# A two-layer graph network on one core: in-degrees, W2's low parts and a score weight placed elsewhere in the order of work

## The chip, the core and the metric

The kernel runs on one core of a Trainium2 chip. The core's engines work side by side, each through its own queue in order: TensorE (PE) for matmuls and transposes, VectorE (DVE), ScalarE (ACT), GpSimd (POOL), and SyncE (SP), which here only issues DMAs. They wait for one another through semaphores. The metric is the device time of one execution in microseconds, lower is better.

## The reference

A graph of 1250 nodes (rows of 768 numbers) and 40000 edges goes through two residual blocks. The first is a graph attention network of two layers, the second a graph convolution network of two layers.

```python
h = relu(layernorm(x))
# layer 1 of the attention network, 4 heads of 512 columns; layer 2: 1 head of 768
def gat(x, W, a_src, a_dst, bias):
    h = (x @ W).reshape(N, H, C)
    e = leaky_relu(al_s[src] + al_d[dst], 0.2)   # al_s = <h, a_src>, al_d = <h, a_dst>
    ex = exp(e - segment_max(e, dst)[dst])
    out = segment_sum(h[src] * (ex / segment_sum(ex, dst)[dst]), dst)
    return out + bias
x = x + gat(elu(gat(h, W1, ...)), W2, ...)
h = relu(layernorm(x))
def gcn(x, W, b):
    h = x @ W
    deg = segment_sum(ones, dst); dinv = where(deg > 0, rsqrt(deg), 0)
    return segment_sum(h[src] * (dinv[src] * dinv[dst])[:, None], dst) + b
x = x + gcn(relu(gcn(h, G1, c1)), G2, c2)
```

Every node has a loop to itself as well. The in-degrees `deg` are needed only by the convolution network, that is in the second half of the kernel.

## The kernel before, in words

The edges become a dense table `counts` of how often each source points to each destination: 10 tiles of 128 sources by 1280 destinations, 16-bit integers. All sums over edges are then matmuls against weights made from this table.

To keep float32 accuracy, every matmul is done three times: each operand is split in a high part (a rounded copy, made by ScalarE) and a low part (the difference, made by VectorE), and high x high, high x low and low x high are added up in PSUM.

The work goes in this order. First x is normalised and multiplied with W1 for all heads (30 row tiles written to memory, the last ten, of head 0, kept on chip). Then come the four heads. A head has five chunks of up to 256 destinations; with q the number of the chunk over all heads (0 to 19), TensorE does for each q the products of chunk q - 2 with W2 (`products`, four pieces: two row tiles by two halves of the columns, in two banks of PSUM, so the third piece waits until VectorE has added the first to the rows), and then the sums over sources of chunk q (`sums`). Between the sums stand two `turn_out` transposes of chunk q - 1, at s = 3 and s = 6; the second waits for the low part of the first, `elu_lo`. The weights of a chunk are made in five groups of two source tiles: ScalarE's `exps`, VectorE's `weigh`, ScalarE's `hi`, VectorE's `lo`, through two buffers and a ring of five slots. VectorE also finds each head's maxima over the masked scores (`take_top`, one instruction a source tile), adds products (`add_products`), divides (`normalize`), finishes elu (`elu_out`, `elu_lo`) and splits W2's rows (`split_weights`: in the second chunk of a head, c = 1, four instructions for W2's four blocks of that head). Head 0 has no earlier head to lie beside, so its maxima are found while TensorE is still at the last ten tiles (`row_lo` and `row_hi` split those); after them TensorE turns the maxima (`turn_top`, after tile 4), the shift (`turn_shift`, after tile 5) and broadcasts it (`spread_first`, after tile 6). `first_slopes` makes the score weights of W2's four blocks for the first head, W2 times the attention vectors.

After the heads comes the second attention layer, made by the same `Weights` object from chunk number `SECOND` = 20 on. Between the layers TensorE has to wait for the first weights of the new layer. Then the convolution network follows.

The in-degrees are nine additions over the tiles of `counts` on VectorE (`degree_sums`), two conversions on ScalarE (`degrees_out`) and 20 matmul records with a column of ones on TensorE (`degrees`, after the last tile); VectorE copies the result to `deg`.

The order on every engine is written out by hand in the program; nothing plans it. All waits are counts on semaphores. Lines: `exps` L250, `weigh` L267 and L269, `hi` L258, `lo` L276, `degree_sums` L1039, `row_lo` L1045, `take_top` L1056 and L1058, `first_slopes` L966, `row_hi` L687, `degrees_out` L698, `degrees` L1469, `split_weights` L716 (ScalarE) and L1101 (VectorE), `normalize` L1114 and L1122, `elu_lo` L1138, `add_products` L1151, `second_lo` L1177, `turn_out` L1517, `sums` L1535, `products` L1565, the second layer's sums L2080.

Of the kernel before, what the change touches and what calls it, by code (L numbers as in the profile page):

```python
# [6 lines left out]
fp32 = mybir.dt.float32  # L7
# [79 lines left out]
class Memory:  # L87

    def __init__(self, nc, keep):
# [50 lines left out]
        self.deg_sum = late("deg_sum", [P, NP], u16)  # L140
# [160 lines left out]
def first_layer(nc, st, mem, x, src, dst, W2, b1, as2, ad2, h_scratch, w_in, a_in, load_weights, load_vectors, tile_in, later):  # L301
# [15 lines left out]
    deg_sum = mem.deg_sum  # L317
    LATE = 3 * G * CW * 4
    deg_f = [Area(nc, mem.at_weights + at + LATE, mem.at_x)(f"deg_f{j}", [P, NP // 2], fp32)
             for j, at in enumerate((WEIGHT_BYTES - RING_BYTES, WEIGHT_BYTES - RING_BYTES // 2))]  # L320
# [99 lines left out]
    b1bc = sbx("b1bc", [P, HA], fp32)  # L420
    w2_st = sbx("w2_st", [P, 2, D], fp32)
    w2 = [sbx("w2_hi", [P, KH, DS], f32r), sbx("w2_lo", [P, KH, DS], f32r)]
    a2bc = sbx("a2bc", [P, 2, D], fp32)
    second = mem.rows_all[:, :, D], al02[:, :, 0]
# [19 lines left out]
    W2v = W2.rearrange("(i p) n -> p i n", p=P)  # L444
    SECOND = HEADS * NC
# [59 lines left out]
    with nc.Block() as block:  # L505
        @block.sync
        def _(sp):
# [44 lines left out]
            for h in range(HEADS):  # L552
# [3 lines left out]
                if h + 1 < HEADS:  # L556
# [9 lines left out]
                    load_bias(h + 1)  # L566
            half.sync(sp)

        @block.gpsimd
        def _(pool_):  # L570
# [38 lines left out]
            pool_.wait_ge(deg_f_ready, 2)  # L609
# [7 lines left out]
        def _(act):  # L617
# [77 lines left out]
            def degrees_out():  # L695
                act.wait_ge(d_step, T - 1)
                for j in range(2):
                    nc.scalar.activation(deg_f[j][:, :], deg_sum[:, j * NP // 2:(j + 1) * NP // 2], ACT.Copy).then_inc(deg_f_ready, 1)  # L698
# [36 lines left out]
            for h in range(HEADS):  # L735
                scores = al[:, :, h], al02[:, :, h]
                for c in range(NC):
                    q = h * NC + c
                    last, second_last = before(q, 1), before(q, 2)
                    for g in range(NG):  # L740
# [5 lines left out]
                        if q == 0 and g == 1:  # L746
                            degrees_out()
                        if q == 0 and g == NG - 1:
                            act.wait_ge(deg_done, 1)
# [20 lines left out]
            for dt in range(NDT):  # L770
                elu_hi(SECOND - 2, dt)

# [25 lines left out]
        def _(dve):  # L798
# [236 lines left out]
            def degree_sums(tiles):  # L1035
                for t in tiles:
                    if t >= 2:
# [28 lines left out]
            for k in range(KH):  # L1066
# [14 lines left out]
            shift_parts(nc, chain, mem, dest_scores(0), lambda: dve.wait_ge(reduced, 1), shift_ready)  # L1081
            row_lo(5)
            dve.wait_ge(shift_t, 1)
            nc.vector.tensor_copy(shiftT[:, 0, :], p_s0).then_inc(shift_out, 1)
            degree_sums(range(1, 5))
            row_lo(6)
            degree_sums(range(5, 7))
# [125 lines left out]
            for h in range(HEADS):  # L1213
                final = h == HEADS - 1
                for c in range(NC):
                    q = h * NC + c
                    last, second_last = before(q, 1), before(q, 2)
                    for g in range(NG - 1):
# [8 lines left out]
                        if q == 0 and g == 0:  # L1227
                            row_lo(T - 3)
                            degree_sums(range(7, T))
                        if g >= 1:  # L1230
                            wt.lo(nc, dve, q, c, g - 1)
                        if second_last is not None and g == 1:
                            elu_lo(second_last, 1)
                        if q == 0 and 1 <= g <= 2:
                            row_lo(T - 3 + g)
                        if q == 0 and g == 2:
                            dve.wait_ge(deg_done, 1)
# [1020 lines left out]
```

## Time and profile before

| | us |
|---|---|
| three runs | 1159.08, 1156.29, 1159.99 (median 1159.08) |
| profiled execution | 1161.38, span 1159.5 |
| TensorE busy (96% of the span) | 1113.2 |
| VectorE busy (73%) | 850.5 |
| ScalarE busy (44%) | 512.3 |
| GpSimd busy (2%) | 27.5 |

The rows further down have the start of an instruction in us from the span's start, its duration, engine, source line and operation, and what it writes and reads. In square brackets stands how long the engine was idle before it, and which instruction released it. A row may merge several instructions (x10). The granted clock is TensorE's, as a share of 2.4 GHz.

### The profile page before, as it was taken

Reading aid. Unit: us, or ns where it says so; the run is one execution under the profiler, and the core shown is the slowest. Engines: PE = TensorE matmul, PEld = TensorE weight load, DVE = VectorE, ACT = ScalarE, POOL = GpSimd, SP = SyncE. Lnnn points to the kernel's source line nnn. Section 1 sums busy time; section 2 is a strip of 40 time slices with the busy share of each in tenths; the row PEclk is TensorE's granted clock in tenths of the full one; section 3 lists DMA queues with packets and bytes.
Section 4 is the critical chain, followed back from the end, with each engine's and each line's share of the span. In section 5 each row is a group of like instructions: output and inputs, shape, how many; then the busy total and the mean of one; then the engine's idle time right before and its main releaser. Section 6 shows DMA issues by size and latency. Waiting matters only on the chain.

```text
span 1159.5 us, 17646 instructions
## 1 busy us (share of the span) xinstructions
PE 1113.2 (96%) x7126; PEld 1044.8 (90%) x7126; DVE 850.5 (73%) x1431; ACT 512.3 (44%) x1056; POOL 27.5 (2%) x40
## 2 busy tenths in 40 slices
PE   5999999988999999999999999989999999999998
PEld 4878886788999999999999999979998999899998
DVE  7998898888879888898879777689777533341263
ACT  4232322276446655575446665255537521431110
POOL 4200000020000000000000000000000000000000
PEclk9999999998999999999999999989999999999999
DMA  6134232021003100201003000031012200100321
GB/s 234 53 120 114 71 128 73 1 64 55 1 29 100 34 23 14 90 25 55 1 28 101 29 1 1 1 123 52 28 56 79 82 1 2 28 14 1 134 83 52
DMA packets 29347, 63.17 MB, mean 54 GB/s; under 512 B 3684, under 2 KB 6344, under 8 KB 29264
## 3 DMA queue, kind: packets, MB, share of 16 engines
q1 hardware_dynamic: 29072, 61.68, 16.5%
q8 instruction: 60, 0.98, 0.3%
q10 hardware_dynamic: 192, 0.32, 0.1%
q14 instruction: 23, 0.19, 0.1%
HBM read 46.45 MB, written 15.54 MB: 53 GB/s over the span
## 4 chain that ended last, share of the span: by engine, by line
PE 68%; DVE 7%; DMA 1%; ACT 1%; issue 1%; DVEq 0%; ACTq 0%
PE banks L1535 20%; PE banks L1565 14%; PE banks L2080 9%; PE banks L2203 6%; PE banks L2196 5%; PE banks L2145 5%; PE banks L2119 4%; PE banks L1517 2%; DVE top L1058 1%; ACT e L250 1%; DMA w_st<-in_L_gnn_W 1%; PE banks L235 1%; DVE pf L269 1%; DVE e L267 1%; DVE w_lo L1101 0%
## 5 line engine op out<-in xcount | busy, mean ns | idle before, releaser
L1535 PE MATMUL banks<-hs,ring_hi 128*128 128x258 f32 (+1 forms) x1600 | 303.0, 290 | 4.3 <-DVE z L1122 4.3
L1535 PEld LDWEIGHTS banks<-hs,ring_hi 128*128 128x128 f32 (+1 forms) x1600 | 250.8, 190 | 6.2 <-DVE z L1122 4.5
L1535 PE MATMUL banks<-hs,ring_lo 128*128 128x258 f32 (+1 forms) x800 | 228.3, 285 | 0.0
L250 ACT ACTIVATE e<-banks,al 128x256 f32<-128x256 f32 (+1 forms) x450 | 180.5, 494 | 8.4 <-PE banks L235 8.4
L258 ACT ACTIVATE ring_hi<-pf 128x512 fp32r<-128x512 f32 (+1 forms) x125 | 81.7, 653 | 173.0 <-DVE pf L269 169.9
L1535 PEld LDWEIGHTS banks<-hs,ring_lo 128*128 128x128 f32 (+1 forms) x800 | 152.0, 190 | 0.0
L1565 PE MATMUL banks<-w_hi,oT_hi 128*128 128x386 f32 (+3 forms) x320 | 109.4, 342 | 3.4 <-DVE shiftT L1211 3.2
L1565 PE MATMUL banks<-w_lo,oT_hi 128*128 128x386 f32 (+3 forms) x320 | 108.7, 340 | 0.0
L1565 PE MATMUL banks<-w_hi,oT_lo 128*128 128x386 f32 (+3 forms) x320 | 108.2, 338 | 0.0
L267 DVE TENSOR_TENSOR e<-e 128x512 f32<-128x512 f32 (+1 forms) x125 | 84.6, 677 | 24.9 <-ACT e L250 24.6
L1409 PE MATMUL banks<-w_hi,xT_hi 128*128 128x512 f32 x240 | 96.7, 403 | 1.3 <-DVE xT_lo L879 0.8
L1409 PE MATMUL banks<-w_hi,xT_lo 128*128 128x512 f32 x240 | 93.7, 390 | 0.0
L1409 PE MATMUL banks<-w_lo,xT_hi 128*128 128x512 f32 x240 | 93.7, 390 | 0.0
L269 DVE SCALAR_TENSOR_TENSOR pf<-e,counts 128x512 f32<-128x512 f32 (+1 forms) x125 | 84.9, 680 | 4.3
L276 DVE TENSOR_TENSOR ring_lo<-pf,ring_hi 128x512 fp32r<-128x512 f32 (+1 forms) x125 | 84.3, 674 | 4.5 <-ACT ring_hi L258 2.1
L891 DVE TENSOR_TENSOR hot<-codes,parts_of 125x1300 bf16<-125x1300 uint16 x97 | 74.0, 827 | 5.2 <-PE banks L1422 5.2
L2080 PE MATMUL banks<-hs_hi,ring_hi 128*128 128x386 f32 x200 | 70.9, 354 | 6.1 <-DVE hs_lo L1177 4.6
L2080 PE MATMUL banks<-hs_lo,ring_hi 128*128 128x386 f32 x200 | 69.2, 346 | 0.0
L2203 PE MATMUL banks<-z_hi,d_hi 128*128 128x384 f32 (+1 forms) x200 | 67.6, 338 | 0.0
L2203 PE MATMUL banks<-z_lo,d_hi 128*128 128x384 f32 (+1 forms) x200 | 67.6, 338 | 0.0
L1151 DVE TENSOR_TENSOR rows<-rows,banks 128x384 f32<-128x384 f32 (+2 forms) x80 | 44.2, 552 | 31.6 <-PE banks L1565 30.7
L2080 PE MATMUL banks<-hs_hi,ring_lo 128*128 128x386 f32 x200 | 66.3, 337 | 0.0
(273 smaller groups left out, 2129.0 us busy)
## 6 DMA issues: line engine op xcount, KB each, us to landing
w_st<-in_L_gnn_W SPq DMA_DIRECT2D x26, 384.0 KB, 3.2
h_scratch<-stage SPq DMA_DIRECT2D x30, 256.0 KB, 2.0
hs<-h_scratch SPq DMA_DIRECT2D x30, 256.0 KB, 2.9
w_st<-in_L_gnn_W SPq DMA_DIRECT2D x4, 1536.0 KB, 7.4
gw_st<-in_L_gnn_W SPq DMA_DIRECT2D x12, 384.0 KB, 4.0
xr<-in_x SPq DMA_DIRECT2D x9, 384.0 KB, 10.2
rows<-in_x SPq DMA_DIRECT2D x9, 384.0 KB, 3.9
x_scratch<-rows SPq DMA_DIRECT2D x9, 384.0 KB
```

What stands on the lines that cost most here:

```text
L250: last = nc.scalar.activation(self.e[:, local % 2, a, i, 0:n], self.p_shift[:, a, 0:n], ACT.Exp, bias=scores[a][:, g * G + i:g * G + i + 1])
L258: nc.scalar.activation(self.ring[0][:, g, :, 0:n], self.pf[:, (c * NG + g) % 2, :, 0:n], ACT.Copy)\
L267: nc.vector.tensor_tensor(e[:, 0], e[:, 0], e[:, 1], ALU.max).then_inc(self.e_max, 1)
L269: nc.vector.scalar_tensor_tensor(out=self.pf[:, local % 2, :, 0:n], in0=e[:, 0], scalar=1.0, in1=counts[:, g * G:(g + 1) * G, d0:d0 + n], ...
L276: nc.vector.tensor_tensor(self.ring[1][:, g, :, 0:n], self.pf[:, (c * NG + g) % 2, :, 0:n], self.ring[0][:, g, :, 0:n].bitcast(fp32), ALU. ...
L891: nc.vector.tensor_tensor(hot[:, wd % SLOTS, :, :, :].rearrange("e a i (v t) -> e (a i) v t", t=2), codes[:, :, :, :].rearrange("e a i (v ...
L1409: last = nc.tensor.matmul(p_h[n % 2], xT[a][:, k, t * P:(t + 1) * P], w[b][:, k, :], start=u == 0, stop=u == 3 * KD - 1)
L1535: last = nc.tensor.matmul(p_a[0:m, dt, half, 0:HH], wt.ring[a][:, s // G, s % G, dt * P:dt * P + m], hs[:, s, b, half * HH:(half + 1) * HH ...
L1565: last = nc.tensor.matmul(p_g[i % 2][0:m, 0:cols.stop - cols.start], oT[a][:, k, dt * P:dt * P + m], w2[b][:, k, cols], start=j == 0, stop ...
L2080: last = nc.tensor.matmul(p_a(t)[0:m, half, 0:AH], wt.ring[a][:, s // G, s % G, dt * P:dt * P + m], hs[b][:, s, half * AH:(half + 1) * AH] ...
L2145: last = nc.tensor.matmul(p_f(f)[:, 0:n], w1[a][:, k, f * P:(f + 1) * P], yT[b][:, k, 0:n], start=u == 0, stop=u == len(terms) - 1)
L2203: last = nc.tensor.matmul(p_q(d)[0:m, half, :], d_hi[0:k, d % 2, s, 0:m], z[a][0:k, s, half * HALF:(half + 1) * HALF], start=s == 0 and a ...
```

## The change

Five edits, all of order and place; the arithmetic is the same.

1. `degree_sums` leaves the first head. Its nine steps stand in chunks 1 to 4 of the last head, between the additions of products (list `DEGREES`). The sums and their float copies lie where the W2 staging and the attention vectors were.
2. `degrees_out` on ScalarE stands behind the heads, `degrees` on TensorE behind the broadcast of the second layer's first shift. VectorE copies the result behind the third weighing of that layer. The waits for them in the first head, on all engines, go; SP waits for the degrees before the second half's loads.
3. `first_slopes` of the fourth block stands behind `shift_parts` and no longer ahead of the maxima.
4. VectorE's `split_weights` for blocks 2 and 3 stands in the third chunk (c = 2, after group 1) and no longer at the end of the second. ScalarE's part stays.
5. GpSimd's memset of the rows no longer waits for the degrees.

```diff
--- before.py
+++ after.py
@@ -137,7 +137,6 @@
         late = Area(nc, self.at_late, end)
         self.abc = late("abc", [P, 2, HID], fp32)
         self.stage = late("stage", [P, 2, HID], fp32)
-        self.deg_sum = late("deg_sum", [P, NP], u16)
         self.junk = edges("junk", [P, 2, HID], bf16)
         self.edges = edges
         self.e_i = edges("e_i", [EP, 2, EJ, EC], i32)
@@ -314,10 +313,6 @@
     stage, junk = mem.stage, mem.junk
     al_row = sbp("al_row", [NV, NP], fp32)
     vr = [sbp("v_hi", [P, KD, NV], f32r), sbp("v_lo", [P, KD, NV], f32r)]
-    deg_sum = mem.deg_sum
-    LATE = 3 * G * CW * 4
-    deg_f = [Area(nc, mem.at_weights + at + LATE, mem.at_x)(f"deg_f{j}", [P, NP // 2], fp32)
-             for j, at in enumerate((WEIGHT_BYTES - RING_BYTES, WEIGHT_BYTES - RING_BYTES // 2))]
     top0 = sbp("top0", [P, NP], fp32)
     early = Area(nc, sbp.at, mem.at_weights + 26 * 1024)
     a2_first = early("a2_first", [P, 2, D], fp32)
@@ -418,9 +413,13 @@
     ev = sbx("ev", [P, NDT, HID], fp32)
     pos = sbx("pos", [P, NDT, HID], fp32)
     b1bc = sbx("b1bc", [P, HA], fp32)
+    at_w2_st = sbx.at
     w2_st = sbx("w2_st", [P, 2, D], fp32)
     w2 = [sbx("w2_hi", [P, KH, DS], f32r), sbx("w2_lo", [P, KH, DS], f32r)]
+    on_a2, on_w2 = Area(nc, sbx.at, sbx.at + 2 * D * 4), Area(nc, at_w2_st, at_w2_st + 2 * D * 4)
     a2bc = sbx("a2bc", [P, 2, D], fp32)
+    deg_sum = on_a2("deg_sum", [P, NP], u16)
+    deg_f = [on_a2("deg_f0", [P, NP // 2], fp32), on_w2("deg_f1", [P, NP // 2], fp32)]
     second = mem.rows_all[:, :, D], al02[:, :, 0]
     second_dest = mem.rows_all[:, :, D + 1], al02[:, :, HEADS]
 
@@ -442,6 +441,7 @@
     a2_early, w2_early = sem("a2_early"), [sem(f"w2_early{k}") for k in range(KH)]
     v2hi_done, v2lo_done = sem("v2hi_done"), sem("v2lo_done")
     W2v = W2.rearrange("(i p) n -> p i n", p=P)
+    DEGREES = [(), (1, 2, 3), (4, 5), (6, 7), (8, 9)]
     SECOND = HEADS * NC
     FIRST_COLS, REST_COLS = slice(0, CW), slice(CW, NP)
     p_first = banks[:, 6, 0:NDT * P].rearrange("p (k c) -> p k c", c=P)
@@ -564,6 +564,7 @@
                         sp.wait_ge(wt.used, (h + 1) * (NC * NG) + (t // G + 1))
                         sp.dma_start(hs[:, t, 1, 0:HID].bitcast(fp32), h_scratch[h + 1, :, t, :]).then_inc(tile_in[t], 16)
                     load_bias(h + 1)
+            sp.wait_ge(deg_done, 1)
             half.sync(sp)
 
         @block.gpsimd
@@ -606,7 +607,6 @@
             nc.gpsimd.memset(b1bc[:, HID:HA], 0.0).then_inc(ones_done, 1)
             for j in range(2):
                 pool_.wait_ge(spilled[j], 16 * (FIRST // 2))
-            pool_.wait_ge(deg_f_ready, 2)
             nc.gpsimd.memset(mem.rows_all[:, :, :], 0.0).then_inc(zeroed, 1)
 
             pool_.wait_ge(hi2_done, 6)
@@ -694,6 +694,7 @@
 
             def degrees_out():
                 act.wait_ge(d_step, T - 1)
+                act.wait_ge(w2lo_done, HEADS * KH)
                 for j in range(2):
                     nc.scalar.activation(deg_f[j][:, :], deg_sum[:, j * NP // 2:(j + 1) * NP // 2], ACT.Copy).then_inc(deg_f_ready, 1)
 
@@ -743,10 +744,6 @@
                             elu_hi(second_last, 0)
                         if q == 0 and g <= 2:
                             row_hi(T - 3 + g)
-                        if q == 0 and g == 1:
-                            degrees_out()
-                        if q == 0 and g == NG - 1:
-                            act.wait_ge(deg_done, 1)
                         if g >= 1:
                             wt.hi(nc, act, q, c, g - 1)
                         if second_last is not None and g == 1:
@@ -769,6 +766,7 @@
                         split_weights(h, range(2, KH))
             for dt in range(NDT):
                 elu_hi(SECOND - 2, dt)
+            degrees_out()
 
             def second_hi(t):
                 act.wait_ge(wt.used, (SECOND + 1) * NG)
@@ -1034,6 +1032,8 @@
 
             def degree_sums(tiles):
                 for t in tiles:
+                    if t == 1:
+                        dve.wait_ge(v2_done, 2 * KH * HEADS)
                     if t >= 2:
                         dve.wait_ge(d_step, t - 1)
                     nc.vector.tensor_tensor(deg_sum[:, :], counts[:, 0, :] if t == 1 else deg_sum[:, :], counts[:, t, :],
@@ -1063,7 +1063,7 @@
                     ins.then_inc(top_step, 1)
                     n_top[0] += 1
 
-            for k in range(KH):
+            for k in range(KH - 1):
                 first_slopes(k)
             row_lo(0)
             dve.wait_ge(al_done, 1)
@@ -1079,12 +1079,11 @@
             dve.wait_ge(top_t, 1)
             nc.vector.tensor_reduce(mem.amax[:, :], p_top0[:, 0:T, :], AX.X, ALU.max).then_inc(reduced, 1)
             shift_parts(nc, chain, mem, dest_scores(0), lambda: dve.wait_ge(reduced, 1), shift_ready)
+            first_slopes(KH - 1)
             row_lo(5)
             dve.wait_ge(shift_t, 1)
             nc.vector.tensor_copy(shiftT[:, 0, :], p_s0).then_inc(shift_out, 1)
-            degree_sums(range(1, 5))
             row_lo(6)
-            degree_sums(range(5, 7))
 
             def split_rows(h, g):
                 if h == 0:
@@ -1226,16 +1225,14 @@
                             elu_lo(second_last, 0)
                         if q == 0 and g == 0:
                             row_lo(T - 3)
-                            degree_sums(range(7, T))
                         if g >= 1:
                             wt.lo(nc, dve, q, c, g - 1)
                         if second_last is not None and g == 1:
                             elu_lo(second_last, 1)
+                        if c == 2 and g == 1:
+                            split_weights(h, range(2, KH))
                         if q == 0 and 1 <= g <= 2:
                             row_lo(T - 3 + g)
-                        if q == 0 and g == 2:
-                            dve.wait_ge(deg_done, 1)
-                            nc.vector.tensor_copy(deg[:, :], p_d).then_inc(deg_done, 1)
                         if c == 0 and 1 <= g <= 2:
                             split_rows(h, g - 1)
                         if c == NC - 1 and not final and g == NG - 2:
@@ -1249,6 +1246,8 @@
                             add_products(second_last, range(1))
                             if c == NC - 2 and not final:
                                 weight_slope(h + 1, 2, 0)
+                            if final:
+                                degree_sums(DEGREES[c][0:1])
                             add_products(second_last, range(1, 2))
                     if c == 0:
                         split_rows(h, 2)
@@ -1256,6 +1255,8 @@
                         weight_slope(h + 1, 3, 0)
                     if not final:
                         next_top(h, c, 0)
+                    else:
+                        degree_sums(DEGREES[c][1:2])
                     if second_last is not None:
                         add_products(second_last, range(2, 3))
                     if c == NC - 1 and not final:
@@ -1264,6 +1265,8 @@
                         next_top(h, c, 1)
                     elif c >= 2:
                         second_top((c - 2) * NDT)
+                    else:
+                        degree_sums(DEGREES[c][2:3])
                     if second_last is not None:
                         add_products(second_last, range(3, NB))
                     if c == 0:
@@ -1278,8 +1281,6 @@
                     wt.lo(nc, dve, q, c, NG - 1)
                     if c == 0:
                         split_rows(h, NG - 1)
-                    if c == 1:
-                        split_weights(h, range(2, KH))
                     if c == NC - 2 and not final:
                         weight_slope(h + 1, 2, 1)
                     if c == NC - 1 and not final:
@@ -1331,6 +1332,8 @@
             second_lo(5)
             wt.lo(nc, dve, SECOND, 0, 1)
             wt.weigh(nc, dve, counts, SECOND, 0, 2)
+            dve.wait_ge(deg_done, 1)
+            nc.vector.tensor_copy(deg[:, :], p_d).then_inc(deg_done, 1)
             second_lo(6)
             second_lo(7)
             dve.wait_ge(top_t, 2 * HEADS + 1)
@@ -1347,6 +1350,7 @@
             second_lo(8)
             wt.lo(nc, dve, SECOND, 0, 4)
             second_lo(9)
+            dve.wait_ge(deg_done, 2)
             half.vector(dve)
 
         @block.tensor
@@ -1464,7 +1468,6 @@
 
             def degrees():
                 pe.wait_ge(deg_f_ready, 2)
-                pe.wait_ge(win_out, len(GROUPS))
                 for t in range(T):
                     last = nc.tensor.matmul(p_d[:, t:t + 1], deg_f[t // (T // 2)][:, t % (T // 2) * P:(t % (T // 2) + 1) * P], ones[:, 0:1].bitcast(fp32),
                                             start=t == 0, stop=t == T - 1)
@@ -1485,7 +1488,7 @@
                 pe.wait_ge(shift_out, 1)
                 wt.broadcast(nc, pe, pick, shiftT[:, 0, :], 0, 0)
 
-            between = {0: score_columns, 4: turn_top, 5: lambda: turn_shift(0, p_s0), 6: spread_first, 9: degrees}
+            between = {0: score_columns, 4: turn_top, 5: lambda: turn_shift(0, p_s0), 6: spread_first}
             for t in range(T):
                 tile(FIRST + t)
                 if t in between:
@@ -1511,8 +1514,6 @@
                 m = rows_of(q % NC * NDT + dt)
                 pe.wait_ge(o_done, q + 1)
                 pe.wait_ge(olo_done, q * NDT + dt)
-                if q == 0 and dt == 0:
-                    pe.wait_ge(deg_done, 2)
                 for f in range(KH):
                     last = nc.tensor.transpose(p_o[:, f, 0:m], z[0:m, dt, f * P:(f + 1) * P], ident[0:m, 0:m])
                 last.then_inc(turned, 1)
@@ -1584,6 +1585,7 @@
             turn_shift(HEADS, p_shift_first)
             pe.wait_ge(shift_out, HEADS + 1)
             wt.broadcast(nc, pe, pick, shiftT[:, 0, :], SECOND, 0)
+            degrees()
 
             def turn_rest():
                 pe.wait_ge(top_ready, HEADS + 2)
```

## Rows read from the trace of the kernel before

**Rows 1.** TensorE's waits over the whole span: line waited for, total us, times, longest

```profile
PE banks L1517 <- DVE oT_lo L1138: 7.8, 3, 3.9
...
PE banks L2080 <- DVE hs_lo L1177: 4.6, 1, 4.6
```

**Rows 2.** time lines around the first maxima: start, us, engine, line, operation, [idle <- releaser]

```profile
195.85 2.39 PE L1462 MATMUL banks<-ident,al_row 8*128 8x8 f32 x20
...
196.86 0.96 DVE L966 CUSTOM_DVE_ANT_0 junk<-w_st,a_first 128x768 bf16<-128x768 f32 x1 [0.17 <-DVE v L966]
...
202.59 0.60 ACT L687 ACTIVATE hs<-banks 128x512 fp32r<-128x512 f32 x1 [6.03 <-PE banks L1409]
...
203.70 0.68 DVE L1045 TENSOR_TENSOR hs<-banks,hs 128x512 fp32r<-128x512 f32 x1
...
216.36 1.31 PE L1476 MATMUL banks<-ident,top 128*128 128x128 f32 x10 [1.57 <-DVE top L1058]
...
223.29 0.81 DVE L1039 TENSOR_TENSOR deg_sum<-counts 128x1280 uint16<-128x1280 uint16 x1
```

**Rows 3.** time lines of the first head's first chunk, columns as in rows 2

```profile
239.39 2.29 PE L1469 MATMUL banks<-ones,deg_f 128*128 128x1 f32 x20
...
239.58 0.60 ACT L687 ACTIVATE hs<-banks 128x512 fp32r<-128x512 f32 x1 [0.25 <-PE banks L1409]
...
240.60 1.56 ACT L250 ACTIVATE e<-banks,al 128x256 f32<-128x256 f32 x4
...
242.19 0.69 DVE L267 TENSOR_TENSOR e<-e 128x512 f32<-128x512 f32 x1
...
261.24 0.53 PE L1535 MATMUL banks<-hs,ring_hi 128*128 128x258 f32 x2 [4.27 <-DVE z L1122]
```

**Rows 4.** time lines, the first head's second chunk ends

```profile
273.73 0.85 ACT L716 ACTIVATE w_hi<-w_st 128x768 fp32r<-128x768 f32 x1 [1.82 <-DMA w_st<-in_L_gnn_W]
...
274.60 0.96 DVE L1101 TENSOR_TENSOR w_lo<-w_st,w_hi 128x768 fp32r<-128x768 f32 x1 [1.71 <-ACT w_hi L716]
...
276.06 0.69 DVE L267 TENSOR_TENSOR e<-e 128x512 f32<-128x512 f32 x1 [0.49 <-ACT e L250]
```

**Rows 5.** time lines, third chunk of the first and of the last head

```profile
281.04 0.69 DVE L267 TENSOR_TENSOR e<-e 128x512 f32<-128x512 f32 x1 [0.42 <-ACT e L250]
...
286.93 0.56 DVE L1151 TENSOR_TENSOR rows<-rows,banks 128x384 f32<-128x384 f32 x1 [0.36 <-PE banks L1565]
...
288.80 0.34 PE L1565 MATMUL banks<-w_hi,oT_hi 128*128 128x384 f32 x1
...
668.72 0.69 DVE L267 TENSOR_TENSOR e<-e 128x512 f32<-128x512 f32 x1 [0.35 <-ACT e L250]
...
674.16 0.54 DVE L1151 TENSOR_TENSOR rows<-rows,banks 128x384 f32<-128x384 f32 x1
...
675.01 0.34 PE L1565 MATMUL banks<-w_hi,oT_hi 128*128 128x384 f32 x1
```

**Rows 6.** time line of VectorE, the last head's second chunk

```profile
652.53 0.56 DVE L1151 TENSOR_TENSOR rows<-rows,banks 98x384 f32<-98x384 f32 x1 [1.54 <-PE banks L1565]
```

**Rows 7.** time lines between the two layers

```profile
743.91 1.58 ACT L777 ACTIVATE hs_hi<-rows 128x768 fp32r<-128x768 f32 x2 [3.70 <-PE banks L1535]
...
767.28 0.63 ACT L258 ACTIVATE ring_hi<-pf 128x512 fp32r<-128x512 f32 x1 [0.64 <-DVE pf L269]
...
768.16 0.66 PE L2080 MATMUL banks<-hs_hi,ring_hi 128*128 128x386 f32 x1 [4.58 <-DVE hs_lo L1177]
```

**Rows 8.** windows: length, busy us per engine, granted clock (PEclk); then one TensorE row

```profile
216.40:222.00 5.60, 5.60 (x30) 4.46 (x30) 2.95 (x8) 0.14 (x1) 0.00 (x0) 1.00 0.00 0
...
410.00:412.00 2.00, 2.00 (x12) 2.00 (x12) 1.34 (x3) 2.00 (x7) 0.00 (x0) 0.56 0.00 0
...
768.20:775.20 7.00, 7.00 (x27) 6.96 (x28) 6.31 (x9) 6.29 (x15) 0.00 (x0) 0.62 0.62 218
...
408.15 0.90 PE L1517 MATMUL banks<-ident,z 128*128 128x128 f32 x4 [1.98 <-DVE oT_lo L1138]
```

## The prediction

> **What bounds the kernel now.** I read the list of TensorE's waits first, then the time lines of the engines around each edited place, then the windows with the granted clock. TensorE is busy for 96% of the span, so only its idle time, or its time at the lower clock, is there to be won. The list of waits [rows 1] gives 7.8 us to three waits for oT_lo and 4.6 us to one wait between the layers. The others that bear on the change are single gaps: 1.57 us for the first head's maxima [rows 2] and 4.27 us for z [rows 3]. The change touches four of these places and adds no matmul: it moves 20.
>
> **Score weights of W2's fourth block behind the shift.** Of `first_slopes`, the last block takes VectorE from 196.86 to 198.74 us, 1.88 us [rows 2]: two fused products (0.96 us each) with their small reads. Without it `row_lo(0)` could start at about 196.7 (ScalarE's part is there by then), and the copy of the scores, which needs TensorE's score columns (20 from 195.85, done at 198.24 [rows 2]), at 198.3 in place of 199.34. Three maxima later the saving of 1.04 us meets `row_lo(1)`. That ran at 203.70 without a wait; its input comes from ScalarE at 202.59 + 0.60 = 203.19 [rows 2]. So it can't start before about 203.21, and of 1.04 us only 0.49 is left. From there the maxima run back to back, and TensorE's wait of 1.57 us before the ten transposes [rows 2] becomes 1.08. Gain 0.49 us; the bounds are 0 and 1.57 (the wait itself). The 1.88 us go behind `shift_parts`, at about 219.8 to 221.8 on VectorE, ahead of `row_lo(5)`, which TensorE wants two tiles later; the first of the removed sums stood at 223.29 [rows 2], so at least as much time comes free right behind. ScalarE's `row_hi(6)` and GpSimd's three small memsets now wait for the moved products, and both are due after 223 us. I take nothing for these.
>
> **In-degrees out of the first head.** Nine sums (0.81 us for the first [rows 2]), some 7.3 us of VectorE, two copies on ScalarE and 20 matmuls of 2.29 us [rows 3] leave. TensorE's sums of the first chunk can start right behind the last tile, 2.1 us sooner. I count nothing for it. The chain does not pass there: ScalarE's last `row_hi`, released by TensorE's last tile, runs at 239.58, then the exponentials of 240.60, and VectorE takes them at 242.19 [rows 3]; from here VectorE works through pairs, low parts and maxima, and TensorE, which finished the chunk at 256.97, idles 4.27 us until 261.24 [rows 3] for z. Finishing sooner lengthens that idle time. ScalarE's order keeps the 242.19 where it is, since `row_hi(9)` stands in front of those exponentials. If the gap were TensorE's own doing, the gain would be 2.1 to 2.3 us; between 0 and 2.3 I take 0, since the gap is twice what moves. SP's and GpSimd's queues lose or gain a wait that ended early already.
>
> **Low parts of W2's second half in the third chunk.** Before, the two instructions (0.96 us each) stood at the end of the second chunk in time in which VectorE had nothing else: it waited 1.71 us before the second, and 0.49 us more for the exponentials [rows 4]. Both waits are ScalarE's, and ScalarE waited 1.82 us for W2's load [rows 4]. The edit leaves ScalarE's order alone, so the exponentials still come at 276.06, and the three waits for oT_lo stay. But 1.8 us now stand in the third chunk, before its third group. In the last head VectorE would have reached that group at 668.37 and waited 0.35 us for it at 668.72 [rows 5]. The low parts (1.74 us start to start) put it at 670.1, 1.38 us late. Normalising and the first product's addition, back to back behind it, move from 674.16 to 675.54, and the addition ends at 676.1. TensorE's third product begins at 675.01 [rows 5] and waits for that addition (two banks of PSUM). Stall: 676.1 - 675.0 = 1.1 us. It is on the path: TensorE waits nowhere else in that stretch. In the first head the same shift is 1.26 us (idle 0.42 at 281.04). The addition could have started at 286.57, when z ended, but waited 0.36 for its product at 286.93, so it moves to 287.8 and ends at 288.4, against a third product at 288.80 [rows 5]: 0.4 us to spare. Heads two and three have somewhat longer idle pieces at the same place and I take 0 there too. The W2 product itself, two products of 2.1 us ahead of 675.01, wants the low parts at 670.8, 0.7 us after they are done. Bounds: 0 below, since VectorE could fill it from idle time nearer by, and 1.1 + 3 x 1.2 = 4.7 us if the margins in the other heads are gone. I take 1.1 us.
>
> **In-degrees in the last head.** The sums stand between the additions. Before the third VectorE waited 1.54 us for its product [rows 6], so 0.81 fits; before the second it waits about 0.5 us in the last head's chunks, so that addition moves by 0.3 us, and its bank is wanted a product (2.1 us) later. The conversions on ScalarE (1.36 us) fall into its idle 3.70 us before 743.91 [rows 7]. Nothing.
>
> **In-degrees between the layers.** Behind TensorE's last broadcast 4.58 us are idle, to 768.16 [rows 7]. The list names hs_lo, but that was long done; what ends the gap is ScalarE's ring_hi, 767.28 + 0.63 = 767.91 [rows 7]. 20 matmuls of 2.29 us fit, with 2.3 us left over. VectorE's copy of the result (0.2 us) stands behind the third weighing; TensorE has no gap there. SP's load of b2's row, and those of x behind it in its queue, wait a few us longer; VectorE reads them only behind the last of its `second_lo`. Cost 0; if the cover were gone it would be 2.3.
>
> The gap has a second price. After it the clock is at the lower of its levels: 0.62 of 2.4 GHz granted as the mean over 768.2 to 775.2 [rows 8], the lower level (1.2 GHz) over most of it. 7.0 x (1 - 0.62) = 2.7 us are lost, with TensorE busy throughout, so all on the path. After the gap of 1.57 us the clock was full (1.00 from 216.4 [rows 8]); after 1.98 us, from 408.15, it was mostly at half (0.56 over 410 to 412 [rows 8]). The idle rest of 2.3 us lies just above, and the matmuls that fill the other half have one column each. So the clock's part is between -2.7 and 0. I take 0, by the nearer row.
>
> The Trainium skill (TensorE: Matmul & The Clock Gate, section "What's actually happening") says that half rate is the default and that recent activity releases it, by a watch that does not start with the kernel. By it the same gap could come out either way from run to run, and by it this part would be 0 in some runs and -2.7 in others; the trace agrees so far that only long gaps are followed by half rate.
>
> **Sum.** -0.5 (maxima) + 0 + 1.1 (last head) + 0 + 0 = +0.6 us. Against the profiled execution (1161.38 us, span 1159.5) that is 1162.0. This execution stands 2.3 us above the median of the three runs, 1159.08, so the time is 1159.7.
>
> **Rivals.**
> - *The clock stays up between the layers.* For: the idle piece halves, and 1.57 us did no harm. Against: 1.98 us did. -2.7 + 0.6 = -2.1: 1157.0 us. Downstream nothing takes it back, as the next chunk's low parts are due more than 2 us before TensorE wants them.
> - *TensorE is the bound in the first head after all*, and its 2.1 us come through, perhaps with the whole 1.57 at the maxima. For: TensorE is busy without a gap up to 256.97. Against: 4.27 us of idle time behind it. -2.1 + 0.6 = -1.5: 1157.6; with the clock as well 1154.9.
> - *Slower: the third product stalls in every head.* Its place is the addition after z in the third chunk; it decides when TensorE reaches the third product more than 0.4 us sooner against VectorE than in this trace. In heads two and three it would, whenever the clock does not fall after the wait for oT_lo: some 3.5 us at 0.56 [rows 8] are worth 1.5 us, all of which TensorE would be sooner. Then stalls of 1.1 us each in two to three heads: +0.6 + 2.2 to 3.3 = +2.8 to +3.9, 1161.9 to 1163.0. Against: in this trace the clock fell in all three.
> - *The low parts cost nothing* and the rest is noise: -0.5, 1158.6.
>
> **How the numbers follow.** Forecast 0.42, clock 0.2, first head 0.1, slower 0.14, low parts free 0.14. The three runs shown lie 3.7 us apart, so a median moves by about 1 us by itself. The range goes from 1155.0 (two of the gains together) to 1162.3. What can be told from no change is about 0.3%, 3.5 us: under 1155.6 or over 1162.6. The first needs clock and first head together, or one of them with a low draw: 0.15. The second needs the stalls of at least two more heads: 0.09. The rest, 0.76, is no change.
>
> **What the new profile would show.** Right: the wait before the ten transposes near 1.1 us; the wait for z above 6 us; the waits for oT_lo as before; a new wait of about 1 us on the third product of the last head's third chunk, released by VectorE's addition; 20 matmuls of one column behind the last broadcast, and half rate after them. Wrong: no such new wait, or waits in all four heads; a granted clock of 1.00 over the seven microseconds after the gap; a wait for z that is shorter than before.

## The result and the profile after

The changed kernel takes 1162.82 us (median of 20 runs, 1160.55 to 1165.15), the kernel before 1159.95 us (20 runs, 1156.29 to 1164.48). The ratio is 1.0024, 95% interval 1.0014 to 1.0035: 2.8 us slower, 1.6 to 4.1. That is less than the 0.3% which the prediction called telling, but it is no longer nothing with 20 runs each, and it lies above the range (1162.3). The profiled execution took 1163.19 us, span 1161.3.

| | before | after |
|---|---|---|
| median, us | 1159.95 | 1162.82 |
| profiled execution (span), us | 1161.38 (1159.5) | 1163.19 (1161.3) |
| TensorE waits for oT_lo, us (times) | 7.8 (3) | 9.4 (4) |
| for the products' addition | none listed | 2.8 (3) |
| for z in the first head | 4.3 (1) | 3.2 (1), and 1.8 (1) for e |
| between the layers | 4.6 (1) | 1.1 (1) |

The first view of the kernel after is the list of TensorE's waits, with the columns of [rows 1].

```profile
PE banks L1518 <- DVE oT_lo L1137: 9.4, 4, 4.2
...
PE banks L1536 <- DVE z L1121: 3.2, 1, 3.2
PE banks L1566 <- DVE rows L1150: 2.8, 3, 0.9
...
PE banks L234 <- ACT e L249: 1.8, 1, 1.8
...
PE banks L1479 <- DVE top L1058: 1.1, 1, 1.1
PE banks L2082 <- DVE hs_lo L1176: 1.1, 1, 1.1
```

The new line is the third: three waits of up to 0.9 us, for an addition of products on VectorE (L1150; L1151 before). The next view is TensorE's time line at these waits and at the waits for oT_lo ahead of them, in heads two, three and four. It answers to [rows 5] and to the last line of [rows 8].

```profile
408.59 0.63 PE L1518 MATMUL banks<-ident,z 128*128 128x128 f32 x4 [2.56 <-DVE oT_lo L1137]
...
418.73 0.41 PE L1566 MATMUL banks<-w_hi,oT_hi 128*128 128x384 f32 x1 [0.93 <-DVE rows L1150]
...
538.08 0.63 PE L1518 MATMUL banks<-ident,z 128*128 128x128 f32 x4 [1.89 <-DVE oT_lo L1137]
...
548.22 0.41 PE L1566 MATMUL banks<-w_hi,oT_hi 128*128 128x384 f32 x1 [0.94 <-DVE rows L1150]
...
666.27 0.63 PE L1518 MATMUL banks<-ident,z 128*128 128x128 f32 x4 [0.68 <-DVE oT_lo L1137]
...
676.41 0.41 PE L1566 MATMUL banks<-w_hi,oT_hi 128*128 128x384 f32 x1 [0.93 <-DVE rows L1150]
```

The windows of the kernel after, 3.5 us behind three gaps of TensorE, show the granted clock (third figure from the end).

```profile
408.60:412.10 3.50, 3.50 (x30) 3.50 (x31) 3.47 (x6) 3.11 (x9) 0.00 (x0) 1.00 0.00 0
538.10:541.60 3.50, 3.50 (x30) 3.50 (x31) 3.47 (x6) 3.11 (x9) 0.00 (x0) 1.00 0.00 0
769.60:773.10 3.50, 3.50 (x12) 3.50 (x13) 3.47 (x6) 2.79 (x7) 0.00 (x0) 0.55 0.87 261
```

In heads two and three the clock is 1.00 behind the wait, though the idle time was 2.56 and 1.89 us. In the profile of before it was 0.56 in the window of [rows 8]. So in head two TensorE reaches the third product sooner than there, finds the addition missing, and starts it at 418.73, the same time as in the profile of before. Two profiles side by side hide the loss: the one lost it to half rate, the other to the wait.

VectorE's time line in the last head's third chunk, the counterpart of 668.72 and 674.16 in [rows 5]:

```profile
668.59 1.82 DVE L1100 TENSOR_TENSOR w_lo<-w_st,w_hi 128x768 fp32r<-128x768 f32 x2
670.32 0.69 DVE L266 TENSOR_TENSOR e<-e 128x512 f32<-128x512 f32 x1
...
675.72 0.54 DVE L1150 TENSOR_TENSOR rows<-rows,banks 128x384 f32<-128x384 f32 x1
```

The low parts stand where the prediction put them, their group of weights comes at 670.32 (forecast 670.1) and the addition at 675.72 (forecast 675.54).

Between the layers, TensorE:

```profile
764.93 3.57 PE L1472 MATMUL banks<-ones,deg_f 128*128 128x1 f32 x20
769.58 0.66 PE L2082 MATMUL banks<-hs_hi,ring_hi 128*128 128x386 f32 x1 [1.08 <-DVE hs_lo L1176]
```

and the granted clock while the 20 matmuls ran:

```profile
765.00:767.00 2.00, 2.00 (x15) 2.00 (x14) 1.90 (x2) 1.96 (x6) 0.00 (x0) 0.73 0.00 0
767.00:768.50 1.50, 1.50 (x8) 1.42 (x7) 1.47 (x3) 1.07 (x3) 0.00 (x0) 0.50 0.00 0
```

They took 3.57 us, not the 2.29 of [rows 3]: about 1 us after they began the clock fell. That is this profile, and not the rule. Six more kernels below have the same 20 matmuls between the layers. In four of them (low parts back, in-degrees alone, addition first, both edits) the clock was full over all 20, which took 2.39 us, and fell in the idle rest of 2.25 us behind. With the high parts moved too it fell as the last of the 20 ended, and with the filler behind the in-degrees about 1 us after they began. The kernel with the in-degrees alone, while the 20 ran:

```profile
759.30:761.60 2.30, 2.30 (x21) 2.25 (x20) 2.20 (x3) 2.25 (x7) 0.00 (x0) 1.00 0.00 0
```

### The profile page after: what moved, and what is told of

The parts are those of the page before. It is cut to its first block, busy times and chain, and to the rows that moved or that the text cites. A ratio compares the mean times of both kernels' runs of the same rounds, so it can differ in the third digit from the quotient of the medians.

```text
span 1161.3 us, 17647 instructions
## 1 busy us (share of the span) xinstructions
PE 1115.0 (96%) x7126; PEld 1045.3 (90%) x7126; DVE 847.7 (73%) x1431; ACT 513.4 (44%) x1056; POOL 27.3 (2%) x40
## 4 chain that ended last, share of the span: by engine, by line
PE 79%; DVE 15%; DMA 3%; ACT 2%; issue 1%; SPq 0%; POOL 0%; DVEq 0%; ACTq 0%; POOLq 0%
PE banks L1536 18%; PE banks L1566 13%; PE banks L1413 11%; PE banks L2082 9%; PE banks L2205 6%; PE banks L2198 5%; PE banks L2147 5%; PE banks L2121 4%; DVE top L1058 2%; PE banks L1426 2%; DVE pf L268 1%; DVE e L266 1%; DMA w_st<-in_L_gnn_W 1%; PE banks L1518 1%; ACT e L249 1%
## 5 line engine op out<-in xcount | busy, mean ns | idle before, releaser
L1536 PE MATMUL banks<-hs,ring_hi 128*128 128x258 f32 (+1 forms) x1600 | 299.9, 288 | 3.2 <-DVE z L1121 3.2
L1536 PEld LDWEIGHTS banks<-hs,ring_hi 128*128 128x128 f32 (+1 forms) x1600 | 248.2, 188 | 5.2 <-DVE z L1121 3.4
L1566 PEld LDWEIGHTS banks<-w_hi,oT_hi 128*128 128x128 f32 (+1 forms) x320 | 59.5, 186 | 10.1 <-issue 5.6
```

The source lines that it names most:

```text
L1536: last = nc.tensor.matmul(p_a[0:m, dt, half, 0:HH], wt.ring[a][:, s // G, s % G, dt * P:dt * P + m], hs[:, s, b, half * HH:(half + 1) * HH ...
L1566: last = nc.tensor.matmul(p_g[i % 2][0:m, 0:cols.stop - cols.start], oT[a][:, k, dt * P:dt * P + m], w2[b][:, k, cols], start=j == 0, stop ...
```

## The experiments

Each of the first four kernels has one part of the change alone or undone. Times are medians of 12 runs where nothing else is said; the kernel before stood at 1159.49 us (35 runs) beside the first four and at 1159.83 (29) beside the next four. Every ratio is to the kernel before. Differences to the changed kernel are between medians of different series; by the ratios, 3.4, 2.6, 5.8 and 11.4 us below would be 3.9, 2.6, 5.5 and 10.8.

### Low parts back

```diff
-                        if c == 2 and g == 1:
-                            split_weights(h, range(2, KH))
...
+                    if c == 1:
+                        split_weights(h, range(2, KH))
```

> The changed kernel with one edit undone: W2's second low parts stand at the end of the second chunk again. Theory (the low parts in the third chunk are the loss, through the first product's addition and so the third product): the time falls back to about 0.5 us under the kernel before, a ratio of 0.9995 to it and 2.5 to 3.3 us under the changed kernel; no wait on add_products is left in TensorE's list. Rival (the in-degrees in the last head and between the layers are the loss): it stays 2 to 3 us above the kernel before, a ratio of 1.002. Rival (the score weights behind the shift): the same 1.002.

1159.45 us, ratio to before 0.9990 (0.9977 to 1.0004): 3.4 us under the changed kernel. The waits on the addition are gone from the list. The loss is in this edit, and both rivals are out.

### Low parts alone

The same two places the other way round, on the kernel before.

> The kernel before with only W2's second low parts moved into the third chunk. Theory (low parts): +2.5 to +3.3 us over the kernel before, with waits on add_products of 0.9 us in the last head always, and in heads 2 and 3 where the clock stays up after the wait for oT_lo. Both rivals: within 0.5 us of the kernel before.

1163.92 us, ratio 1.0035 (1.0022 to 1.0048): 4.1 us slower (2.6 to 5.6), a little over the upper end of what was expected. TensorE's time line has the wait in heads three and four:

```profile
547.90 0.41 PE L1565 MATMUL banks<-w_hi,oT_hi 128*128 128x384 f32 x1 [0.92 <-DVE rows L1151]
...
676.05 0.41 PE L1565 MATMUL banks<-w_hi,oT_hi 128*128 128x384 f32 x1 [0.92 <-DVE rows L1151]
```

In head two, where the clock was 0.65 of full over 3.5 us behind the wait for oT_lo, there is none: the third product starts at 418.62 and the addition, begun at 417.51, is done by 418.1. That is the theory's own exception: a margin of about half a microsecond, near the 0.4 that the prediction had read in the first head, and like it behind a stretch at half rate.

### Score weights alone

```diff
-            for k in range(KH):
+            for k in range(KH - 1):
                 first_slopes(k)
...
+            first_slopes(KH - 1)
             row_lo(5)
```

> The kernel before with only the fourth block's score weights behind the shift. Theory: the wait before the ten transposes falls from 1.57 to 1.1 us and the time by 0.5 us, too little to see in the time. Rival (this edit is the loss, by holding up row_lo and the shift behind it): +2 to +3 us and a new wait of TensorE between 217 and 240 us.

1160.28 us, ratio 1.0006 (0.9992 to 1.0020). The wait before the transposes is 1.10 us, as forecast; the half microsecond can't be seen in the time. No new wait came up behind it:

```profile
216.84 1.31 PE L1477 MATMUL banks<-ident,top 128*128 128x128 f32 x10 [1.10 <-DVE top L1058]
...
261.70 0.51 PE L1536 MATMUL banks<-hs,ring_hi 128*128 128x258 f32 x2 [2.77 <-DVE z L1123]
```

The wait for z is 2.77 us, not the 4.27 of before, though this edit does not touch it. Behind the 20 matmuls of one column in the first head, which here end at about 242 us, the clock fell with no idle time of TensorE before it:

```profile
243.25:246.25 3.00, 3.00 (x16) 3.00 (x15) 2.97 (x4) 1.86 (x5) 3.00 (x1) 0.50 0.98 336
```

In the same place it was 1.00 in the profile of before. Of the five profiles with these matmuls in the first head it fell in three (low parts alone, score weights alone, the best version), and in these three the wait for z is 2.8 us; in the other two it is 4.3. So the wait for z takes up most of what the half rate costs.

This profile also has heads two and three at the full clock without the low parts in the way, which gives the price of the wait. Third head, from the transposes behind the wait for oT_lo to the products that wait for shiftT:

```profile
536.87 0.63 PE L1518 MATMUL banks<-ident,z 128*128 128x128 f32 x4 [1.70 <-DVE oT_lo L1139]
...
593.72 0.45 PE L1566 MATMUL banks<-w_hi,oT_hi 128*128 128x384 f32 x1 [1.06 <-DVE shiftT L1212]
```

| third head | start, end | us | clock behind the start |
|---|---|---|---|
| before | 538.00, 596.42 | 58.42 | 0.51 |
| score weights alone | 536.87, 593.72 | 56.85 | 1.00 |
| after | 538.08, 596.11 | 58.03 | 1.00 |

The wait of 0.94 us costs 58.03 - 56.85 = 1.18 us. Half rate costs 1.57. With the low parts alone the same stretch is 57.99 us, also at the full clock and with the wait.

### In-degrees alone

The edits to `degree_sums`, `degrees_out`, `degrees`, their memory and their waits, without the other two.

> The kernel before with only the in-degrees moved (last head, and between the layers). Theory (low parts): 0 to -0.3 us, the 20 matmuls lie in the idle piece between the layers and the granted clock falls while they run, as in the changed kernel. Rival (in-degrees): +2 to +3 us, the nine sums delay additions in the last head and TensorE waits for them, or the first weights of the second layer come later against the last broadcast.

1159.38 us, ratio 0.9991 (0.9975 to 1.0008). The rival that blames the in-degrees is out. One thing expected did not come: the clock was 1.00 while the 20 matmuls ran and fell only in the idle rest. From the third head's wait to the first matmul of the second layer this kernel takes 763.89 - 533.68 = 230.21 us, the kernel before 768.16 - 538.00 = 230.16: the nine sums and the 20 matmuls are hidden, and gain nothing either. The clock behind the third head's wait was near half rate in both (0.57 and 0.51).

### The first product added before normalising

If the low parts cost only through that addition, moving the addition ahead must heal it while they stay.

```diff
                     else:
+                        if c == 2:
+                            add_products(second_last, range(1))
                         if last is not None:
                             normalize(last)
                         if second_last is not None:
-                            add_products(second_last, range(1))
+                            if c != 2:
+                                add_products(second_last, range(1))
```

> The changed kernel with one more edit: in each head's third chunk VectorE adds the first product before it normalises, and no longer after. The low parts stay in the third chunk. Theory (the low parts cost time only because they push the first addition behind TensorE's third product): the waits on add_products (0.93 us in heads 2 to 4) go, and the time falls by 2.5 to 4 us to that of the kernel before or 0.5 us under it. Rival (the low parts cost time by some other way, such as later weights or a later load of W2's next rows): the waits on add_products go but the time stays within 1 us of the changed kernel.

1160.21 us, ratio to before 1.0002 (0.9988 to 1.0016), 2.6 us under the changed kernel. The second head shows it at the full clock: from the transposes behind the wait for oT_lo to the products that wait for shiftT it takes 56.86 us, where the changed kernel takes 58.04. The list of waits has no line for the addition, and the line for oT_lo is unchanged:

```profile
PE banks L1521 <- DVE oT_lo L1137: 9.3, 4, 4.3
```

### High parts too

The waits for oT_lo are TensorE's largest inside the heads. ScalarE stands before the load of W2's rows [rows 4] with the next chunk's exponentials and `elu_hi` queued behind.

```diff
                         if second_last is not None and g == 0:
                             elu_hi(second_last, 0)
+                        if c == 2 and g == 0:
+                            split_weights(h, range(2, KH))
...
-                    if c == 1:
-                        split_weights(h, range(2, KH))
```

> The changed kernel with ScalarE's high parts of W2's second half moved as well, behind the first group and elu_hi of the third chunk. Theory (TensorE's wait for oT_lo is ScalarE standing in front of the load of W2's rows): the three or four waits for oT_lo (9.4 us in all) shrink to under 3 us, and with them the half-rate stretches behind; TensorE then reaches the third product still sooner, so the waits on add_products grow to 1 to 2.5 us a head and give a part back. Net -3 to -6 us against the changed kernel. Rival (VectorE's queue sets the pace of these chunks): the waits for oT_lo turn one for one into waits on add_products, net 0.

1157.02 us, ratio 0.9977 (0.9965 to 0.9990): 5.8 us under the changed kernel. The waits for oT_lo are gone, and the waits for the addition have grown as the theory wanted, to 1.4 us in three heads; in the last it is 0.6:

```profile
PE banks L1566 <- DVE rows L1150: 4.9, 4, 1.4
PE banks L1566 <- DVE shiftT L1210: 3.2, 3, 1.1
...
PE banks L1566 <- DVE w_lo L1100: 1.1, 3, 0.7
```

The last line is new: the products now wait a little for the low parts themselves, 0.7 us in the first head.

### Both

> Both edits together on the changed kernel: ScalarE's high parts in the third chunk, and the first product added before normalising. Theory: waits for oT_lo under 3 us and waits on add_products under 1 us in all, -6 to -10 us against the changed kernel, -3 to -7 against the kernel before, clearly below both. Rival: VectorE is the bound here, time within 1.5 us of the kernel before.

1151.37 us (6 runs), ratio 0.9931 (0.9911 to 0.9951): 8.0 us under the kernel before and 11.4 under the changed one, more than expected. The waits for oT_lo and for the addition are gone from TensorE's list. Inside the heads those for shiftT are left (3.2 us in three), those for w_lo (1.1 in three), and in the first head 3.2 for z and 1.8 for e. Each edit alone had left the other's wait.

### Filler between the layers

```diff
             wt.broadcast(nc, pe, pick, shiftT[:, 0, :], SECOND, 0)
+            for _ in range(18):
+                nc.tensor.matmul(banks[:, 2, :], w2[0][:, 0, 0:P], w2[0][:, 1, 0:512], start=True, stop=True)
```

> The kernel before with 18 matmuls of 512 columns in the idle piece between the layers, into a bank that the next sums clear; nothing uses their result. Theory (the half-rate stretch after that piece is a cost of its own): granted clock 1.00 after the piece in place of 0.50 over the first 3.5 us, and -2.3 us in time, if the matmuls (0.22 us each, 4.0 in all) end before 768.2. Rival (VectorE sets the pace of the second layer's first chunk, so a faster clock is waited away): clock 1.00, but new waits, and the time within 0.7 us of the kernel before.

1156.86 us, ratio 0.9977 (0.9959 to 0.9995): 2.7 us gained (0.6 to 4.8), by work that has no use but to keep TensorE busy. From the last broadcast between the layers to the first matmul behind the wait for cr_hi (L2121; L2119 before) the profile takes 131.46 us, where before takes 133.88: 2.4 us less. Time line and window:

```profile
764.19 4.47 PE L1588 MATMUL banks<-w_hi 128*128 128x512 f32 x18
768.85 0.41 PE L2082 MATMUL banks<-hs_hi,ring_hi 128*128 128x386 f32 x1 [0.19 <-DVE hs_lo L1177]
```

```profile
768.90:772.40 3.50, 3.50 (x20) 3.50 (x21) 3.47 (x6) 2.79 (x8) 0.00 (x0) 1.00 0.72 260
```

Against 0.50 in the kernel before:

```profile
768.20:771.70 3.50, 3.50 (x11) 3.50 (x12) 3.46 (x6) 2.79 (x7) 0.00 (x0) 0.50 0.76 283
```

### Filler behind the in-degrees

Nine such matmuls behind `degrees()`, on the kernel with both edits.

> The kernel with both edits (high parts too, first product added first) on the changed kernel, with 9 filler matmuls of 512 columns behind the 20 of the in-degrees. If matmuls of one column do not keep the clock up, it falls while they run, in about as many cases as without filler; the granted clock over the 3.5 us behind is 0.5 to 0.7 and the time stays within 1 us of the kernel without filler. If the idle rest of 2.25 us was what let the clock fall, the clock is 1.00 and the time 2.3 us lower.

1151.22 us (6 runs) against 1151.37 without filler. The ratios of the two series, 0.9921 (0.9899 to 0.9942) and 0.9931 (0.9911 to 0.9951), are too wide to tell no gain from 2.3 us by themselves. The clock had fallen while the in-degrees' matmuls ran, before the filler began:

```profile
756.49 4.19 PE L1593 MATMUL banks<-w_hi 128*128 128x512 f32 x9
```

```profile
756.00:759.00 3.00, 3.00 (x9) 2.52 (x10) 2.93 (x6) 2.26 (x6) 0.00 (x0) 0.50 0.20 76
```

Nine matmuls take 4.19 us here, 18 took 4.47 above. Behind the filler the clock was up again, and not at 0.5 to 0.7 as expected:

```profile
761.00:764.50 3.50, 3.50 (x21) 3.50 (x21) 3.15 (x6) 3.50 (x9) 0.00 (x0) 1.00 1.02 395
```

But at half rate the nine reach beyond the idle rest. The second layer's first sums start 7.44 us after the first of the 20 matmuls (760.48 - 753.04), in the kernel without filler 4.65 (756.77 - 752.12). What the sums gain in clock they lose in start: from the last broadcast to the matmul behind the wait for cr_hi it is 134.30 us with this filler and 134.23 without. So this run says that such a filler is worth nothing once the clock has fallen ahead of it. What it would do where the clock is still full, as in most of the profiles with the 20 matmuls, it does not show.

### The best version

In-degrees in the first head as before, and all that helped: score weights behind the shift, both halves of the split in the third chunk, the addition first, 18 fillers.

> The kernel before (in-degrees in the first head) with the score weights behind the shift, both halves of W2's second split in the third chunk, the first product added before normalising, and the 18 filler matmuls between the layers. If the gains add up: -8.5 us (as with both edits on the changed kernel) and -2.5 us (filler) from the kernel before, 1148.5 to 1150 us. If the in-degrees' new place is worth something by itself (TensorE's 2.1 us in the first head), it is 1 us or more slower than that sum.

1148.72 us (5 runs) beside 1160.71 for the kernel before (11 runs), ratio 0.9901 (0.9882 to 0.9921). It beats the kernel before by 12 us or 1%, and by the ratios the changed kernel by more. The forecast sum of the single gains fits; a worth of its own of the in-degrees' new place did not show, and the interval (9.2 to 13.7 us) would hide one of a microsecond.

## Why the prediction was wrong, step by step

**Score weights: right.** 1.57 became 1.10 us (forecast 1.08), for the reason given, and the time shows nothing.

**In-degrees out of the first head: right in the sum, not in the form.** From the transposes to the first matmul behind the wait for z it took 44.88 us before and 44.81 after. But z's wait did not grow over 6 us: it fell to 3.16, with a new wait of 1.78 for the exponentials ahead of a broadcast, and half rate behind that (0.74 over 3.5 us). TensorE spread its surplus over three places. The prediction had named a shorter wait for z as a sign of being wrong, and that sign did appear; the chain it described, ending in z, still set the time.

**Low parts: the step that failed.** The last head went as written: addition 0.2 us from the forecast place, a wait of 0.93 us, and 1.13 us more from there to the last broadcast (666.27 to 764.35, 98.08 us; before 665.97 to 762.92, 96.95). The step that failed is "Heads two and three have somewhat longer idle pieces at the same place and I take 0 there too". They wait 0.93 and 0.94 us there. The margin had been read off a profile in which TensorE had just run at half rate. Behind the wait for oT_lo in heads two and three the clock stayed full in 8 of the 16 cases of eight profiles (before, after, the four single edits, addition first, filler), and in all three of these cases that have the low parts in the third chunk and the addition behind normalising, TensorE waits 0.92 to 0.94 us. So the edit costs 1.13 us in the last head, and 1.2 us more in each of heads two and three where the clock stays up: 1.1 to 3.5 us, about 2.3 at even odds. The first head would add another 1.2 if its clock stayed up, which no profile with this arrangement shows. Measured: 2.8 (1.6 to 4.1) in the changed kernel, 4.1 (2.6 to 5.6) alone. This was the slower rival, priced at 1161.9 to 1163.0 and given 0.14. Its condition stood in the text, but its chance was set by one profile: three low clocks out of three were read as the rule. One reading was slightly off as well: with 1.74 us for the low parts and 0.42 of idle time the first head's shift is 1.32 us, not 1.26, and its margin 0.35, which changes nothing.

**In-degrees in the last head: right.** No wait comes from them.

**In-degrees between the layers: right.** They stay hidden even at 3.57 us. In five of the seven profiles with them they take 2.39 us and leave an idle rest of 2.25, as forecast. The clock's part is 0, as taken: in all six without filler the clock is 0.50 to 0.55 over the 3.5 us behind the gap. From the last broadcast to the matmul behind the wait for cr_hi these six take 132.9 to 134.2 us, and the three kernels with neither in-degrees nor filler there 133.8 to 134.2. The reason given, the idle rest of 2.3 us, holds in four of the profiles. In the changed kernel's own and in the one with filler behind them the clock had fallen while the 20 ran, and in the first head it fell behind them with no idle time at all. The Trainium skill (TensorE: Matmul & The Clock Gate, section "What's actually happening") says that the throttled state is the default and that activity releases it. The trace fits that and shows what lay in the gap: with idle time alone, or 20 matmuls of one column and idle time, the clock behind it was 0.50 to 0.55, with 18 matmuls of 512 columns it was 1.00 in both kernels that have them.

**The base.** The three runs shown had a median of 1159.08, twenty of them 1159.95. That is a draw of the runs. Of the 3.1 us between forecast and result 0.9 is this, and 2.2 are left for the low parts in heads two and three. Their waits account for 1.2 at even odds and for 2.4 when both heads keep the full clock, as in the profile; the interval of the result (1.3 us to either side) does not tell these apart. Why the low parts alone stand at 4.1 us stays open: 2.3 lies just under its interval (2.6 to 5.6), and only with both heads at the full clock, 3.5, does the account fall inside. Its profile had 0.66 of full clock over 3.5 us behind a wait of 2.63 us at 913.19, and before had 1.00 at 911.60 behind 2.01, a difference that no edit touches.

## What to carry to other kernels

Work moved into an engine's busy stretch has to be held against the next thing that another engine wants from that queue, and the margin must be read where that other engine was at its full clock. When a queue is late by a little, look for the one instruction in it that is waited for and take it to the front, before moving the bulk. The idle piece between the layers cost twice, once as idle time and once at half rate behind it. 18 matmuls of 512 columns that filled it took away the second cost, and 20 matmuls of one column did not.

## What was not expected of the hardware

- Matmuls of one column did not hold the clock. It fell to 0.50 while 20 of them ran in two of seven profiles (changed kernel, filler behind the in-degrees), and behind them in the first head, with no idle time between, in three of five.
- Gaps of like length fell on either side. Of TensorE, 1.98 us had 0.53 behind it in one profile and 2.56 us had 1.00 in another; the first head's wait for z was 3.16 us in both the changed kernel and the one with the in-degrees alone, with 1.00 behind it in one and 0.55 in the other.
- A wait listed as 0.93 us cost 1.13 to 1.18 us of time between two fixed points.
